# Cross-attention and gated feed-forward kernel: projections moved between a slot's score halves, a third projection bank, and softmax sums that share a bank and are added in SBUF

## Chip, core and metric

The kernel runs on one core of one Trainium2 chip, as one launch. The metric is device time in microseconds (us), from one launch to its end. The reference's numbers are fp32 throughout; there is no other core and no collective.

The engines are named as in the profile: PE (TensorE matmuls), PEld (its weight loads), DVE (VectorE), ACT (ScalarE), POOL (GpSimd) and SP (SyncE, which issues DMAs).

## The reference, cut to what matters

`x` is 4 batches of 256 tokens of 128 numbers, `ctx` 4 batches of 512 context rows of 128 numbers. Two layers follow each other for each batch.

```python
# layer 1: cross attention, 16 heads of 64
lat = layer_norm(layernorm(x)); ctx = layer_norm(context)
q = lat @ Wq                       # 256 x 1024
k, v = split(ctx @ Wkv)            # 512 x 1024 each
k = apply_rope(k, cos, sin)
attn = softmax(clip(q @ k.T * 64**-0.5, -11, 11))   # per head, 256 x 512
x = x + (attn @ v) @ Wo + bo

# layer 2: per-token attention over 16 heads of 8, then 8 gated experts
h = rmsnorm(layernorm(x)); q = h @ Wq + bq; kv = (h @ Wdown + bdown) @ Wup + bup
att = softmax(einsum('bthd,btgd->bthg', q, k) / sqrt(8))
y = layernorm(x) + (att @ v) @ Wo + bo
x = x + y + sum_e gate_e(h2) * (h2 @ We[e])         # h2 = rmsnorm(y)
```

## The kernel before

**Work and slots.** A slot is one pair of heads of one batch: 4 batches of 8 pairs give slots 0 to 31; p is the slot's number in its batch. Every engine has its own program, written out over the same list of slots (from -3 to 32), and semaphores tie them. Nothing is scheduled by a planner; the order is what the loops write, plus small tables (`POST_STEPS`, `OWN_STEPS`, `PREP_STEPS`) which say in which slot and at which place in it the steps of the second layer and the preparation of the next batch stand.

**One slot on PE.** With s the slot: `keys(s+3)` (three 512-column matmuls, K below), `scores(s, 0)` (12 matmuls on half the array's rows each, the first two of four context chunks), `queries(s+1)` (three 256-column matmuls, Q), in even slots `sums(s-1)` (16 matmuls of the softmax weights of two pairs with a column of ones), `scores(s, 1)`, `values(n)` (three 512-column matmuls, V; one unit in p = 1 to 4, two in p = 6 and 7, none in p = 0 and 5), and `times_values(s-1)` (8 matmuls, weights times values, called pv below). At places "a" (before Q), "b" (after V) and "c" (at the end) a side product can stand: `norm0` to `norm3`, `out_proj`, `h_T`, `query_down`, `keyval2`, `o_T`, `out_proj2`, `h2_T`, `gate`, `moe0` to `moe3` of the batch before, `ctx_T` and `lat_T` of the next.

**One slot on the others.** ACT takes the exponential of each score half (`exps`), both halves of which use the same two banks `sc`; so the second half's scores wait for the first half's exponential. It also copies queries (`query_hi`), values, rotated keys (`key_hi`) and pv (`attention_copy`, into `u`). POOL adds the rotary halves (`rotate`) and clips the exponentials (`clip`). DVE multiplies the key projection by sine and cosine (`key_products`, first in its slot), and makes the low parts `query_lo` and `key_lo` of the pair for the next slot; `scores(s+1, 0)` waits for both. Between the product with the sine and `rotate` SP issues four DMAs that swap halves.

**The second layer** of batch b runs beside the slots of batch b+1. From `keyval2` (p = 4) to `o_T` (p = 0 of the next batch) it is elementwise work on DVE and POOL: `products`, `sum_logits`, `less_maximum`, `weighted_values`, `reduce_outputs`. `o_T` on PE waits for it.

**Banks.** PSUM has eight banks here: `side`, two of `sc`, `own_bank`, two projection banks `pj_k`, `pv` and `sums`. K, Q and V units take the two projection banks in turn (`PLACE[...] % 2`), and `bank_free` waits for the reader of the unit two before. `sums` gathers the sums of four pairs of a batch's slots in one accumulation of 64 matmuls; `reciprocals(b)` on DVE reads them from there.

After slot 32 the last batch's second layer stands alone (`last_batches`, `TAIL_STEPS`); these last 54 us are called the tail.

Of the kernel before, what the change touches and what calls it, by code (L numbers as in the profile page):

```python
# [210 lines left out]
def xattn_ffn(nc, x, ctx, cos, sin, ln_lat_g, ln_lat_b, ln_ctx_g, ln_ctx_b, Wq, Wkv, Wo, bo,  # L211
              gamma1, f_Wq, f_bq, f_Wdown, f_bdown, f_Wup, f_bup, f_Wo, f_bo, gamma2, f_Wg, f_bg, f_We, out):
    es = ExitStack()
    with es:
# [73 lines left out]
        moe = sb("moe", [128, TT, NE, D])  # L288
        rec = sb("rec", [128, NT])
# [41 lines left out]
        first_value_banks = sc_bank + [pv_bank, sum_bank]  # L331
        side_banks = [pb("side")] + sc_bank + [own_bank] + pj_k + [pv_bank, sum_bank]
# [40 lines left out]
        s_u = sem("s_u")  # L373
        s_rec = sem("s_rec")
# [133 lines left out]
        def _(pe):  # L508
# [1106 lines left out]
```

## Time and profile before

| | us |
|---|---|
| median of 3 runs | 353.66 |
| lowest and highest | 352.28, 353.86 |
| profiled execution, its time | 351.67 |
| its span (first to last instruction) | 349.9 |
| mean granted TensorE clock | 0.943 |

| engine | busy us | share | instructions |
|---|---|---|---|
| PE | 299.8 | 86% | 2472 |
| DVE | 252.7 | 72% | 470 |
| POOL | 206.8 | 59% | 206 |
| ACT | 155.4 | 44% | 287 |

The share is a mean over stages: in slots 25 to 31 PE is busy almost throughout, between `keyval2` and `o_T` DVE is, and in the tail neither. The profile's chain of waits (the work that ended last, followed back) gives each piece its own share of the end, with the overlap of neighbouring matmuls taken off; the timeline gives start and full duration of each instruction. So a matmul of 400 ns in the timeline can be 230 ns of the chain.

### The profile page before, as it was taken

The page shows a single profiled execution, that of the slowest core. Times are in us where ns is not written, and L with a number is a line of the kernel's source. Part 1 is how long each engine was busy: PE and PEld are TensorE (multiplying, and loading weights), DVE is VectorE, ACT ScalarE, POOL GpSimd, SP SyncE. Part 2 cuts the span into 40 slices and gives each one's busy share as a digit, 9 for nine tenths or more (in the row PEclk, how much of TensorE's full clock was granted, in tenths as well). Part 3 has the DMA queues.
Part 4 walks back from the last instruction along what each step waited for, and adds up shares of the span by engine and source line. Part 5 has one row for each costly group of instructions (what it writes and reads, how often), then busy time and mean ns, then how long its engine had stood idle before and what let it go on. Part 6 is the DMA issues. An engine that isn't in the chain of part 4 may idle for free.

```text
span 349.9 us, 6553 instructions
## 1 busy us (share of the span) xinstructions
PE 299.8 (86%) x2472; PEld 198.7 (57%) x2472; DVE 252.7 (72%) x470; ACT 155.4 (44%) x287; POOL 206.8 (59%) x206
## 2 busy tenths in 40 slices
PE   6768999999999999959999999949999999740862
PEld 6545666666686655636776556627776555620331
DVE  3957635435866489997938689996456697799977
ACT  3536454565434545533336475624425665020420
POOL 4527744544656486773755586982544788754661
PEclk9989999999999999998999999978999999995668
DMA  8843212211111111111101020111101000000001
GB/s 230 232 120 81 51 30 63 61 31 34 30 32 32 30 33 32 31 30 32 32 7 42 13 51 11 32 31 32 32 17 46 15 2 3 15 0 0 0 2 30
DMA packets 16318, 14.23 MB, mean 41 GB/s; under 512 B 4832, under 2 KB 11808, under 8 KB 16288
## 3 DMA queue, kind: packets, MB, share of 16 engines
q1 hardware_dynamic: 15232, 13.69, 15.0%
q8 instruction: 20, 0.33, 0.4%
q10 hardware_dynamic: 1056, 0.13, 0.2%
q14 instruction: 10, 0.08, 0.1%
HBM read 4.89 MB, written 0.52 MB: 15 GB/s over the span
## 4 chain that ended last, share of the span: by engine, by line
PE 61%; DVE 26%; ACT 6%; issue 3%; DMA 2%; POOL 1%; SPq 0%; ACTq 0%; DVEq 0%; POOLq 0%
PE pv L587 16%; PE sc L573 14%; PE sums L603 6%; PE pj_k L511 6%; ACT e L794 5%; DVE o L1299 5%; PE pj_k L513 3%; PE pj_k L512 3%; PE side L674 3%; DVE att L1146 2%; DVE o L1302 2%; DVE ks L984 2%; DVE prod L967 2%; DMA sin_in<-in_L_xattn_sin_dram 2%; PE side L718 2%
## 5 line engine op out<-in xcount | busy, mean ns | idle before, releaser
L1488 POOL TENSOR_SCALAR e<-e 128x1024 f32<-128x1024 f32 x64 | 68.9, 1077 | 75.9 <-ACT e L794 68.3
L794 ACT ACTIVATE e<-sc 128x1024 f32<-128x1024 f32 x64 | 65.7, 1027 | 80.8 <-PE sc L573 80.8
L573 PE MATMUL sc<-qs,ks 64*128 64x256 f32 x768 | 63.1, 297 | 6.7 <-ACT e L794 6.0
L573 PEld LDWEIGHTS sc<-qs,ks 64*128 64x128 f32 x768 | 50.1, 187 | 29.4 <-issue 17.6
L587 PE MATMUL pv<-e,v 128*64 128x256 f32 x512 | 65.5, 400 | 0.0
L1481 POOL TENSOR_TENSOR krot<-kcos,kswap 128x512 f32<-128x512 f32 x32 | 41.2, 1288 | 17.0 <-DMA kswap<-ksin 8.9
L587 PEld LDWEIGHTS pv<-e,v 128*64 128x64 f32 x512 | 35.2, 142 | 24.4 <-issue 8.9
L1048 DVE TENSOR_TENSOR ksin<-pj_k,sinT 128x512 f32<-128x512 f32 x32 | 22.1, 690 | 34.6 <-PE pj_k L513 30.7
L984 DVE TENSOR_TENSOR ks<-krot,ks 128x512 fp32r<-128x512 f32 x32 | 33.4, 1043 | 0.0
L802 ACT ACTIVATE u<-pv 128x256 f32<-128x256 f32 x32 | 12.3, 385 | 43.4 <-PE pv L587 43.4
L603 PE MATMUL sums<-e,sum_rows 128*32 128x256 f32 x512 | 30.9, 382 | 0.0
L967 POOL TENSOR_TENSOR prod<-att,kv 128x1024 f32<-128x1024 f32 x8 | 23.4, 2937 | 6.6 <-ACT att L888 6.2
L959 POOL TENSOR_TENSOR prod<-q,kv 128x1024 f32<-128x1024 f32 x8 | 19.5, 2448 | 5.6 <-DVE kv L1179 3.5
L771 ACT ACTIVATE ks<-krot 128x512 fp32r<-128x512 f32 x32 | 20.1, 627 | 4.9 <-POOL krot L1481 4.9
L1048 DVE TENSOR_TENSOR kcos<-pj_k,cosT 128x512 f32<-128x512 f32 x32 | 21.8, 681 | 0.0
L984 DVE TENSOR_TENSOR qs<-pj_k,qs 128x256 fp32r<-128x256 f32 x32 | 13.4, 420 | 11.3 <-ACT qs L777 11.3
L603 PEld LDWEIGHTS sums<-e,sum_rows 128*32 128x32 f32 x512 | 15.0, 109 | 11.0 <-POOL e L1488 0.8
L1299 DVE TENSOR_REDUCE o<-prod 128x64 f32<-128x1024 f32 x16 | 18.8, 1207 | 0.1
L511 PE MATMUL pj_k<-ctxT,wkA 128*128 128x512 f32 x32 | 16.0, 501 | 3.0 <-DVE kcos L1048 2.8
L786 ACT ACTIVATE v<-pj_k 128x512 f32<-128x512 f32 x28 | 16.6, 594 | 1.9 <-PE pj_k L513 1.6
L1530 POOL TENSOR_TENSOR moe<-moe 128x512 f32<-128x512 f32 (+2 forms) x18 | 15.4, 854 | 2.7 <-ACT moe L869 1.8
L967 DVE TENSOR_TENSOR prod<-own_bank,kv 128x1024 f32<-128x1024 f32 x8 | 15.4, 1932 | 0.1
(257 smaller groups left out, 535.4 us busy)
## 6 DMA issues: line engine op xcount, KB each, us to landing
kswap<-ksin SPq DMA_DIRECT2D x128, 64.0 KB, 2.0
ctx_in<-in_ctx_dram SPq DMA_DIRECT2D x4, 256.0 KB, 3.0
prod<-in_L_xattn_Wkv_dram SPq DMA_DIRECT2D x2, 512.0 KB, 6.1
x_in<-in_x_dram SPq DMA_DIRECT2D x1, 512.0 KB, 6.0
prod<-in_L_xattn_Wq_dram SPq DMA_DIRECT2D x1, 512.0 KB, 6.8
wo<-in_L_xattn_Wo_dram SPq DMA_DIRECT2D x1, 512.0 KB, 8.3
fwe<-in_L_ffn_We_dram SPq DMA_DIRECT2D x1, 512.0 KB, 4.8
out_dram<-x_in SPq DMA_DIRECT2D x3, 128.0 KB, 1.8
```

The costliest lines, as they stand in the source:

```text
L511: nc.tensor.matmul(out_ap, w_hi, m_hi, start=True, stop=False)
L573: last = nc.tensor.matmul(sc[:, h, c * NT:(c + 1) * NT], ks[rows, j % 3, k_part, chunk], qs[rows, j % 2, q_part, :], start=(k_part + q_par ...
L587: last = nc.tensor.matmul(pv_bank[DH * h:DH * h + DH, 0:NT], v[:, c, col:col + DH], e[:, j % 3, h, c, :], start=(c == 0), stop=(c == SC - 1))
L603: last = nc.tensor.matmul(sum_bank[32 * g:32 * g + 32, 0:NT], w, e[:, (j - 1 + g // 2) % 3, g % 2, c, :], start=(p == 1 and c == 0), stop= ...
L771: nc.scalar.activation(ks[:, j % 3, 0, :], krot[:, j % 2, :], ACT.Copy).then_inc(s_khi, 1)
L794: nc.scalar.activation(e[:, j % 3, :, 2 * half:2 * half + 2, :].rearrange("p h c n -> p h (c n)"), sc[:, :, :], ACT.Exp, scale=SCALE).then ...
L967: return engine.tensor_tensor(prod[:, t, 1024 * hh:1024 * hh + 1024].rearrange("p (h d g) -> p h d g", h=G // 2, d=GD), weights(t)[:, 8 * ...
L984: return nc.vector.tensor_tensor(dst, whole, f(hi), ALU.subtract)
L1048: nc.vector.tensor_tensor(dst[:, j % 2, :], key_bank(j)[:, :], trig[:, :], ALU.mult).then_inc(s_kmul, 1)
L1299: return nc.vector.tensor_reduce(outputs(t)[:, 8 * hh:8 * hh + 8, :], pr, AX, ALU.add)
L1481: nc.gpsimd.tensor_tensor(krot[:, j % 2, :], kcos[:, j % 2, :], kswap[:, j % 2, :], ALU.add)\
L1488: nc.gpsimd.tensor_scalar(a, a, EXP_HIGH, EXP_LOW, ALU.min, ALU.max).then_inc(s_clip, 1)
```

## The change

- On PE a slot's order becomes `scores(s, 0)`, then in p = 0 `sums(s-1)`, then K, side "a", Q, V, side "b", `scores(s, 1)`, pv, in the other even slots `sums(s-1)`, side "c".
- ACT follows: values and side "b" are taken before the second exponential.
- There are three projection banks (`% 3`), and `bank_free` looks three units back. The first batch's fourth value unit uses `own_bank` and waits until `lat_T` is taken from it.
- `sums` no longer has a bank: it writes the other half of the pv bank (`sum_part`), one accumulation of 16 matmuls each. ACT copies each result to SBUF (`sums_copy`, into `sums_in`), 16 copies of 128x256. PE waits for that copy before the next pv or sums, and in odd pairs `attention_copy` waits for the sums that stand behind pv.
- POOL adds the second and third of a batch's four sums to the first (`add_sums`, in p = 5 and 7, 8 in all). DVE adds the fourth and takes the reciprocal from SBUF.

PE's program in slot 2, an even slot, before: K, first scores (L573), Q, sums, second scores, and the first row of V:

```order
52 L511 MATMUL pj_k<-ctxT,wkA 128x512
53 L512 MATMUL pj_k<-ctxT,wkA 128x512
54 L513 MATMUL pj_k<-ctxT,wkA 128x512
55 L573 MATMUL sc<-qs,ks 128x256 x12
56 L511 MATMUL pj_k<-latT,wqS 128x256
57 L512 MATMUL pj_k<-latT,wqS 128x256
58 L513 MATMUL pj_k<-latT,wqS 128x256
59 L603 MATMUL sums<-e,sum_rows 32x256 x16
60 L573 MATMUL sc<-qs,ks 128x256 x12
61 L511 MATMUL pj_k<-wvS,ctxT 128x512
```

The same slot on PE after the change, from the first scores (L579) to the sums (L614), with the middle of V left out:

```order
51 L579 MATMUL sc<-qs,ks 128x256 x12
52 L515 MATMUL pj_k<-ctxT,wkA 128x512
53 L516 MATMUL pj_k<-ctxT,wkA 128x512
54 L517 MATMUL pj_k<-ctxT,wkA 128x512
55 L515 MATMUL pj_k<-latT,wqS 128x256
56 L516 MATMUL pj_k<-latT,wqS 128x256
57 L517 MATMUL pj_k<-latT,wqS 128x256
58 L515 MATMUL pj_k<-wvS,ctxT 128x512
...
61 L579 MATMUL sc<-qs,ks 128x256 x12
62 L595 MATMUL pv<-e,v 64x256 x8
63 L614 MATMUL pv<-e,sum_rows 32x256 x16
```

All full-array products now stand together between the two halves, and sums stand behind pv.

PE's program in slot 16 before, where `o_T` (the transposes of o) waits for DVE's second layer:

```order
262 L603 MATMUL sums<-e,sum_rows 32x256 x16
263 L573 MATMUL sc<-qs,ks 128x256 x12
264 L610 MATMUL side<-ident,o 128x128 x2
265 L587 MATMUL pv<-e,v 64x256 x8
266 L705 MATMUL side<-fwo,oT 128x128 x2
267 L511 MATMUL pj_k<-ctxT,wkA 128x512
```

And the same place after:

```order
261 L517 MATMUL pj_k<-latT,wqS 128x256
262 L621 MATMUL side<-ident,o 128x128 x2
263 L579 MATMUL sc<-qs,ks 128x256 x12
264 L595 MATMUL pv<-e,v 64x256 x8
265 L714 MATMUL side<-fwo,oT 128x128 x2
266 L579 MATMUL sc<-qs,ks 128x256 x12
```

The second score half of the slot moves from ahead of the waiting transposes to behind them.

POOL's program from slot 31 on after the change (clips, an addition of sums, then a product of the second layer); before, the clips were followed by the product:

```order
151 L1514 TENSOR_SCALAR e<-e 128x2x512 x2
152 L1518 TENSOR_TENSOR sums_in<-sums_in 128x256
153 L991 TENSOR_TENSOR prod<-att,kv 128x1024
154 L1562 TENSOR_TENSOR moe<-moe 128x512
155 L1562 TENSOR_TENSOR moe<-moe 128x256
```

One addition stands ahead of the product that DVE's last addition of sums meets.

```diff
@@ PE, the loop over slots
             for slot in range(-KEYS_AHEAD, AFTER):
+                if 0 <= slot < NPAIR:
+                    scores(slot, 0)
+                if slot > 0 and slot % PAIRS == 0:
+                    sums(slot - 1)
                 if slot + KEYS_AHEAD < NPAIR:
                     keys(slot + KEYS_AHEAD)
-                if 0 <= slot < NPAIR:
-                    scores(slot, 0)
                 side_at(slot, "a")
                 if 0 <= slot + 1 < NPAIR:
                     queries(slot + 1)
-                if 2 <= slot <= NPAIR and slot % 2 == 0:
-                    sums(slot - 1)
-                if 0 <= slot < NPAIR:
-                    scores(slot, 1)
                 for n in value_units(slot):
                     values(n)
                 side_at(slot, "b")
+                if 0 <= slot < NPAIR:
+                    scores(slot, 1)
                 if 1 <= slot <= NPAIR:
                     times_values(slot - 1)
+                if 2 <= slot < NPAIR and slot % 2 == 0 and slot % PAIRS:
+                    sums(slot - 1)
                 side_at(slot, "c")
@@ PE, times_values
                 if j:
                     pe.wait_ge(s_u, j)
+                if j > 1:
+                    pe.wait_ge(s_sums_copied, (j + 1) // 2 if p == PAIRS - 1 else j // 2)
@@ PE, sums
-                if p == 1 and b:
-                    pe.wait_ge(s_rec, b)
+                pe.wait_ge(s_u, j)
+                if j > 1:
+                    pe.wait_ge(s_sums_copied, j // 2)
@@ PE, bank_free
-                if PLACE[kind, n] < 2:
+                if PLACE[kind, n] < 3:
                     return
-                kind, n = PROJECTIONS[PLACE[kind, n] - 2]
+                kind, n = PROJECTIONS[PLACE[kind, n] - 3]
@@ ACT
+            def sums_copy(j):
+                act.wait_ge(s_sum, j // 2 + 1)
+                if j >= PAIRS:
+                    act.wait_ge(s_rec, j // PAIRS)
+                nc.scalar.activation(sums_in[:, j % PAIRS // 2, :], sum_part, ACT.Copy).then_inc(s_sums_copied, 1)
             def attention_copy(j):
                 act.wait_ge(s_pv, j + 1)
+                if j % 2 and j % PAIRS != PAIRS - 1:
+                    act.wait_ge(s_sum, j // 2 + 1)
@@ DVE
             def reciprocals(b):
-                dve.wait_ge(s_sum, PAIRS // 2 * (b + 1))
-                nc.vector.reciprocal(rec[:, :], sum_bank[:, 0:NT]).then_inc(s_rec, 1)
+                dve.wait_ge(s_sums_added, 2 * b + 2)
+                dve.wait_ge(s_sums_copied, PAIRS // 2 * (b + 1))
+                own(nc.vector.tensor_tensor(rec[:, :], sums_in[:, 0, :], sums_in[:, 3, :], ALU.add))
+                nc.vector.reciprocal(rec[:, :], rec[:, :]).then_inc(s_rec, 1)
@@ POOL
+            def add_sums(b, i):
+                pool.wait_ge(s_sums_copied, PAIRS // 2 * b + i + 1)
+                nc.gpsimd.tensor_tensor(sums_in[:, 0, :], sums_in[:, 0, :], sums_in[:, i, :], ALU.add)\
+                    .then_inc(s_sums_added, 1)
+                pool.wait_ge(s_sums_added, 2 * b + i)
@@ POOL, in each slot, behind the second clip
+                if 0 <= b < NB and p in (5, 7):
+                    add_sums(b, p // 2 - 1)
```

## Rows read from the trace of the kernel before

**Rows 1.** Busy time by stage: start:end, length, PE, PEld, DVE, ACT, POOL, PEclk, DMA.
```profile
25.18:95.00 69.82, 66.56 (x611) 44.30 (x612) 38.23 (x77) 37.42 (x61) 37.05 (x35) 0.99 0.20 50
95.00:122.90 27.90, 27.33 (x253) 19.42 (x253) 16.08 (x38) 12.81 (x21) 15.07 (x18) 1.00 0.12 29
122.90:156.40 33.50, 28.08 (x264) 18.07 (x263) 32.11 (x40) 16.26 (x28) 24.96 (x17) 1.00 0.13 32
196.00:233.40 37.40, 31.73 (x271) 19.42 (x271) 34.38 (x40) 20.63 (x44) 30.78 (x25) 0.98 0.12 29
233.40:293.20 59.80, 58.93 (x513) 39.13 (x513) 41.10 (x71) 29.18 (x55) 34.79 (x35) 0.96 0.08 21
293.20:350.00 56.80, 31.01 (x152) 17.91 (x152) 46.77 (x100) 11.01 (x37) 32.13 (x36) 0.77 0.03 8
```

**Rows 2.** Chain that ended last, slots 2 to 7: start us, us, engine, tile, line.
```profile
37.77 0.32 PE pj_k L511
38.32 1.86 PE sums L603 x32
40.18 0.91 PE sc L573 x12
41.09 0.43 PE pj_k L511
41.99 1.88 PE pv L587 x16
...
44.75 0.93 PE sc L573 x10
45.70 1.03 ACT e L794
46.78 0.98 PE sc L573 x12
...
66.82 0.12 PE pj_k L511
...
70.83 0.23 PE pj_k L511
```

**Rows 3.** Timeline, DVE, POOL and PE in the stretches 123 to 156 and 196 to 233 us.
```profile
127.98 0.42 DVE L984 TENSOR_TENSOR qs<-pj_k,qs 128x256 fp32r<-128x256 f32 x1 [0.55 <-ACT qs L777]
148.67 2.91 POOL L967 TENSOR_TENSOR prod<-att,kv 128x1024 f32<-128x1024 f32 x1
149.00 2.73 DVE L1302 TENSOR_TENSOR o<-o,aden 128x128 f32<-128x128 f32 x1
156.39 0.60 PE L610 MATMUL side<-ident,o 128*128 128x128 f32 x2 [3.75 <-DVE o L1302]
206.60 0.69 DVE L1048 TENSOR_TENSOR ksin<-pj_k,sinT 128x512 f32<-128x512 f32 x1 [0.96 <-PE pj_k L513]
233.42 0.66 PE L610 MATMUL side<-ident,o 128*128 128x128 f32 x2 [4.73 <-DVE o L1302]
```

**Rows 4.** Busy time and granted clock (behind POOL's figure) behind the first of PE's two waits.
```profile
157.00:160.50 3.50, 3.50 (x18) 1.90 (x19) 2.84 (x4) 0.52 (x2) 1.95 (x2) 0.59 0.02 5
```

**Rows 5.** Timeline, DVE in slot 19: first key product and low part of the keys.
```profile
181.45 0.69 DVE L1048 TENSOR_TENSOR ksin<-pj_k,sinT 128x512 f32<-128x512 f32 x1 [1.71 <-PE pj_k L513]
185.53 1.55 DVE L984 TENSOR_TENSOR ks<-krot,ks 128x512 fp32r<-128x512 f32 x1
```

**Rows 6.** Timeline, slots 0 and 1: a cast on DVE, scores that wait for ACT.
```profile
26.39 0.68 DVE L1400 CAST spread<-u 128x1024 fp32r<-128x1024 f32 x1
30.13 0.97 PE L573 MATMUL sc<-qs,ks 64*128 64x256 f32 x12 [0.31 <-ACT e L794]
```

**Rows 7.** Timeline, end of the slots: clip and product on POOL, reciprocal on DVE.
```profile
292.49 1.04 POOL L1488 TENSOR_SCALAR e<-e 128x1024 f32<-128x1024 f32 x1 [1.10 <-ACT e L794]
293.61 2.89 POOL L967 TENSOR_TENSOR prod<-att,kv 128x1024 f32<-128x1024 f32 x1
296.23 1.76 DVE L1060 RECIPROCAL rec<-sums 128x256 f32<-128x256 f32 x1 [1.94 <-PE sums L603]
```

More of the change, by code:

```diff
@@ L288, in xattn_ffn @@
         moe = sb("moe", [128, TT, NE, D])
+        sums_in = sb("sums_in", [128, PAIRS // 2, NT])
         rec = sb("rec", [128, NT])
@@ L321, in xattn_ffn @@
         own_bank = pb("own_bank")
-        pj_k = [pb(f"pj_k{i}") for i in range(2)]
+        pj_k = [pb(f"pj_k{i}") for i in range(3)]
         pv_bank = pb("pv")
-        sum_bank = pb("sums")
+        sum_part = pv_bank[:, NT:2 * NT]
         q2_bank = own_bank[:, 0:D]
         att_bank = own_bank[:, NT:2 * NT].rearrange("p (h g) -> p h g", h=G)
-        first_value_banks = sc_bank + [pv_bank, sum_bank]
-        side_banks = [pb("side")] + sc_bank + [own_bank] + pj_k + [pv_bank, sum_bank]
+        first_value_banks = sc_bank + [pv_bank, own_bank]
+        side_banks = [pb("side")] + sc_bank + [own_bank] + pj_k[0:2] + [pv_bank, pj_k[2]]
         ld = {n: sem(f"ld_{n}") for n in ("wk", "trig", "x", "wv", "wq", "bias", "wo", "ffn")}
@@ L373, in xattn_ffn @@
         s_u = sem("s_u")
+        s_sums_copied = sem("s_sums_copied")
+        s_sums_added = sem("s_sums_added")
         s_rec = sem("s_rec")
@@ L436, in value_bank @@
         def value_bank(n):
-            return first_value_banks[n] if value_units_at_first(n) else pj_k[PLACE["values", n] % 2]
+            return first_value_banks[n] if value_units_at_first(n) else pj_k[PLACE["values", n] % 3]
         def key_bank(j):
-            return pj_k[PLACE["keys", j] % 2]
+            return pj_k[PLACE["keys", j] % 3]
         def query_bank(j):
-            return pj_k[PLACE["queries", j] % 2]
+            return pj_k[PLACE["queries", j] % 3]
         def weights(t):
@@ L551, in values @@
                     pe.wait_ge(s_wv, 1)
+                if n == 3:
+                    pe.wait_ge(*taken("lat_T", 0))
                 if not value_units_at_first(n):
@@ L602, in sums @@
                     for g in range(4):
-                        last = nc.tensor.matmul(sum_bank[32 * g:32 * g + 32, 0:NT], w,
+                        last = nc.tensor.matmul(sum_part[32 * g:32 * g + 32, :], w,
                                                 e[:, (j - 1 + g // 2) % 3, g % 2, c, :],
-                                                start=(p == 1 and c == 0), stop=(p == PAIRS - 1 and c == SC - 1))
+                                                start=(c == 0), stop=(c == SC - 1))
                 last.then_inc(s_sum, 1)
@@ L638, in side_product @@
                     pe.wait_ge(s_u, NPAIR)
-                elif k == 7:
-                    pe.wait_ge(s_rec, NB)
-                elif k >= 4:
+                elif k >= 4 and k != 6:
                     pe.wait_ge(s_qlo, NPAIR)
@@ L914, in _ @@
                     exps(slot, 0)
+                if slot > 0 and slot % PAIRS == 0:
+                    sums_copy(slot - 1)
                 side_taken(slot, "a")
@@ L917, in _ @@
                     query_hi(slot + 1)
+                for n in value_units(slot):
+                    value_copy(n)
+                side_taken(slot, "b")
                 if 0 <= slot < NPAIR:
                     exps(slot, 1)
-                for n in value_units(slot):
-                    value_copy(n)
                 if 0 <= slot + KV_AHEAD < NPAIR:
                     key_hi(slot + KV_AHEAD)
-                side_taken(slot, "b")
                 if 1 <= slot <= NPAIR:
                     attention_copy(slot - 1)
+                if 2 <= slot < NPAIR and slot % 2 == 0 and slot % PAIRS:
+                    sums_copy(slot - 1)
                 second_layer(slot, "c")
```

2 lines of the change are left out of this document (1 added, 1 removed).

## Prediction, made blind

> **What bounds the kernel now.** I read the busy time by stage first. From 25 to 123 us and from 233 to 293 us PE is busy nearly throughout (66.56 of 69.82, 27.33 of 27.90, 58.93 of 59.80 us) and DVE well below it [rows 1]. In two stretches, 123 to 156 and 196 to 233 us, it is the other way round: DVE is busy 32.11 of 33.50 and 34.38 of 37.40 us, and at their end PE stands idle for 3.75 and 4.73 us in front of `o_T` [rows 1, 3]. So there are two regimes: slots that PE bounds (2 to 12, 17 to 20, 25 to 31) and two stretches that DVE bounds (13 to 16, 21 to 24). A change on PE pays in the first only. The tail (293 to 350 us, PE 31 of 57 us, DVE 47) is a chain over DVE, PE and ACT which the change leaves alone but for its first link.
>
> Then I read the chain of waits inside PE's slots, for what a slot costs there [rows 2]. First scores 0.91, pv 1.88, sums 1.86. A full-array projection costs 0.43+0.23+0.23=0.89 behind scores or pv, but 0.69 behind another full-array product (its first matmul falls from 0.43 to 0.23). Q costs 0.32+0.12+0.12=0.56 behind scores and 0.36 behind another product. In odd slots nothing but Q lies between the halves, and PE waits for the exponential: 46.78 less 45.68 us, which is 1.10 us, the exponential's 1.03 among it, and then 0.98 for the second half.
>
> **The change on PE's slots.** Even slot before: K 0.89, scores 0.91, Q 0.56, sums 1.86, scores 0.91, V 0.89, pv 1.88, in all 7.90. After: scores 0.91, K 0.89, Q 0.36, V 0.69, scores 0.91, pv 1.88, sums 1.86, in all 7.50: a gain of 0.40. Odd slot before: 0.89+0.93+1.10+0.98+0.89+1.88=6.67. After: the projections (1.94) cover the exponential, 0.91+0.89+0.36+0.69+0.91+1.88=5.64: a gain of 1.03. Slot 5 has no V: 0.82, K and Q (1.25) still covering the 1.10. With two V: 1.04. With p=0: 0.20. Slot 9 has norms in the old gap, which is thus half used: 0.61. Slot 10 has a side product behind pv already: 0.19.
>
> The gain in 0.20 steps is a count of how often PE goes from full-array matmuls to half- or part-array ones: seven changes in an even slot, five after. The Trainium skill, TensorEngine Tiling (Array Packing), Key Properties, says that changing the tiling mode drains the engine. By that rule the new neighbours pv and sums, which tile differently, cost a drain too. The trace shows sums at 1.86 behind a full-array product, where such a change is in it already, so the sum is the same by both; the pair pv, sums itself stands in no row.
>
> Slots 2 to 11: 0.40+1.03+0.40+0.82+0.40+1.04+0.20+0.61+0.19+1.04, which is **-6.1**.
>
> Slots 0 and 1: K(3) used to lie ahead of the first scores, in a wait. Now DVE gets it only after them; its products (1.3), the cast (0.68 [rows 6]), `query_lo` and `key_lo` (1.1) follow one another, and scores(1, 0) starts at about 31.1 instead of 30.13 [rows 6]: **+0.9** with what slot 1 saves again.
>
> **The stretches that DVE bounds.** DVE works in order, and its slot begins with `key_products(s+3)`, which now wait for a K that stands behind the first scores. `keyval2` comes sooner, but DVE then waits for K(16) at the head of slot 13, so nothing of that is kept: +0.3. Inside, waits for Q fall away (0.55 in slot 13 [rows 3] and 0.23 in slot 15) and PE is never late. Stretch 1: **-0.8**. Stretch 2 has such a gap of 0.96, a wait for K [rows 3], and two more for Q of together 1.4; half of the 2.4 goes: **-1.2**. Bounds for each: nothing, and -2.0 if also the 2.73 us of DVE's small product (L1302, which ends as POOL's 2.91 us product does [rows 3]) shrinks.
>
> **Behind `o_T`.** PE now waits with the second scores of the slot still to do. Before, `o_T` 0.6, pv, `out_proj2` and K followed; now `o_T`, scores, pv, `out_proj2`: +0.2 at full clock. The granted clock behind the wait was 0.59 of full, mostly its lower level of 1.2 GHz, until about 160.5 us [rows 4]; PE idled 3.75 us before that. The wait gets longer (about 6 us), and the work in the low clock now counts scores too: the slot after begins at 162.2 to 162.8 instead of 160.96. **+1.5** and, behind the second wait, **+1.3**; bounds 0.2 and 2.5 each.
>
> **Slots 17 to 20 and 25 to 28.** Here DVE is loaded as well. In slot 19 from the first key product to `key_lo` it takes 185.53+1.55-181.45=5.63 us [rows 5]. K is ready 1.8 us after a slot's start (0.7 before), plus 0.1, so a slot with this chain lasts at least 7.55. Slot 19 took 7.28 and gets +0.3; slot 27 took 6.84 with the same chain and gets +0.7; in slot 11 the chain is 4.5, and the slot keeps its gain. Slots 17 to 20: -0.61-0.19+0.3, **-0.5**. Slots 25 to 28: -0.61-0.19+0.7-0.40, **-0.5**.
>
> **Slots 29 to 32.** No K stands here. Slot 29 gains 0.8 (`moe0` moves into the gap). Slot 30 loses what sums used to cover: Q's 0.56 is all there is against 1.10, +0.6. Slot 31 stays. In slot 32 sums no longer stand behind `moe3`, but need the last clip (1.04 us, its exponential ahead of it [rows 7]); then a copy (0.39, as u's) and DVE's addition (0.42, as its 128x256 sums): the reciprocal could start 0.1 later than 296.23. **-0.1** in all.
>
> **The new work.** 16 copies on ACT (6.2 us; ACT is at half load): copies of u and sums behind sums(s-1) end 0.85 us later, while scores(s+1, 0) take 0.91, so the next exponential is not held. 8 additions on POOL of 0.73 each; POOL's product in slot 15 ended some 2 us before DVE needed it, so they are hidden; without that cover they would cost up to 0.7 per stretch. DVE's three inner additions lie in slots 8, 16 and 24, off PE's path. The last does not: POOL's product ran from 293.61 for 2.89 us [rows 7], starts 0.7 later behind `add_sums` and lasts to 297.2. The small DVE product of [rows 3] shows what an operation of DVE with two SBUF inputs does under such a product: it ended when the product did. So the addition, due at 295.8, ends about 1.2 later: **+1.2**, bounds 0 and 1.5. The Trainium skill, SBUF — State Buffer, Who interferes with whom, states it as a rule: DVE with two SBUF inputs contends with a GpSimd instruction that reads SBUF. It speaks against this change, and the trace agrees. With no such contention the sum would be 1.2 better.
>
> **Waits that it adds.** pv waits for the copy of the sums before; it comes 3.7 us after it. The second of two V waits for the key products of its own slot: 0.2 where DVE is free, hidden where it is not. `sums` of slots 16 and 24 now stand ahead of K and need a clip behind POOL's 3 us product: K is still there before DVE asks.
>
> **Sum:** +0.9-6.1-0.8+1.5-0.5-1.2+1.3-0.5-0.1+1.2 is -4.3 us. Against the profiled execution: span 349.9 to 345.6, its time 351.67 to 347.4. The median stands 2.0 above that execution, so I forecast **349.4**.
>
> **Rivals.**
> - *DVE's stretches and the last addition go well.* Both stretches gain their 2.0, the addition finds POOL free, the clock recovers as before: -1.2-2.0-1.5=-4.7 more, **344.7**. For: gaps of that size are there. Against: DVE is at 96% in the first. Chance 0.18.
> - *PE's whole gain arrives.* The same arithmetic for all 32 slots gives -13.5, **340.2**. It needs DVE's stretches to shrink with PE's, against 32.11 of 33.50 us busy. Chance 0.05.
> - *Slower: K comes too late for DVE.* Where DVE's chain from K to `key_lo` is longer than the slot less 1.8 us, the slot grows. I count that for slots 19 and 27. There are ten other loaded slots (9 to 12, 17, 18, 20, 25, 26, 28); each that tips over turns about -0.5 into +0.7. From five on the kernel is at **355.4** and slower; all ten give 361. The chain has 4.5 us against 6.45 in slot 11, and slots 10, 12, 18, 20 are longer still, which is against it; that DVE has 0.2 to 0.9 us more in some of them under POOL's additions speaks for it. Chance 0.11.
> - *The change does little:* low clock after more of the waits in the stretches (up to +2.5 each) with the rest as summed, near **353**. For: PE idles more and in more places there. Chance 0.14.
>
> **How the numbers follow.** The forecast holds 0.52, its own range 346.5 to 352. The range 344 to 355.5 leaves out the full gain and most of the slower rival. A measurement of this kernel can tell about 0.5% (1.8 us) from no change: 351.9 and 355.4 are the borders. Faster 0.71 (forecast most of it, the first two rivals), same 0.16 (the little one and the forecast's upper end), slower 0.13.
>
> **What would show it.** In the profile after: no wait of the second scores for the exponential in slots 2 to 29; odd slots of some 5.7 us and even ones of 7.5 in slots 2 to 8; the start of slot 12 about 5.2 us earlier; `o_T` waits longer than 3.75 and 4.73 us, at 150.5 and about 227 us; a reciprocal that starts 3 to 4 us earlier than 296.23 behind an addition of about 1.5 us. It is wrong if the odd slots do not shorten, if PE's waits for `ks` spread over many slots, or if the low clock is seen away from `o_T`.

## The result and the profile after

| | before | after |
|---|---|---|
| median, us | 353.65 (4 runs) | 360.22 (4 runs) |
| lowest and highest | 352.28, 353.86 | 359.20, 362.31 |
| ratio, 95% interval | | 1.0198, 1.0165 to 1.0230 |
| span of the profiled run | 349.9 | 360.5 |
| mean granted clock | 0.943 | 0.917 |

The kernel became 2% slower, 10.8 us above the forecast and 4.7 above the range. The profiled execution of after is its slowest; the spans of the other three are 357.4, 357.5 and 359.3 us. What is said of stages below holds for the profiled executions.

The table sets the profiled executions side by side. A stage is measured from first scores to first scores; the second and third columns are after less before, as the prediction's sum had it and as measured.

| stage | before, us | forecast | measured |
|---|---|---|---|
| slots 0, 1 | 11.61 | +0.9 | +3.38 |
| 2 to 5 | 28.69 | -2.65 | -2.72 |
| 6, 7 | 16.13 | -1.44 | -0.26 |
| 8 | 7.00 | -0.20 | -0.18 |
| 9 to 11 | 26.84 | -1.84 | +1.16 |
| 12 to 15 (DVE's stretch 1) | 32.89 | -0.8 | +1.05 |
| 16 (behind `o_T`) | 13.24 | +1.5 | +1.59 |
| 17 to 20 | 37.14 | -0.5 | +2.47 |
| 21 to 24 (stretch 2, `o_T`) | 40.59 | +0.1 | -1.83 |
| 25 to 28 | 35.81 | -0.5 | +1.85 |
| 29 to the tail's first norm | 24.36 | +1.1 | +1.79 |
| tail | 50.4 | 0 | +2.2 |

The forecast's two stretches end at the transposes of `o_T`, inside slots 16 and 24. Cut there, slots 12 to 16 up to the transposes came out at +2.03 (forecast -0.8) and what is behind them at +0.61 (forecast +1.5); slots 21 to 24 up to the transposes at -1.88 (forecast -1.2) and what is behind them at +0.05 (forecast +1.3). So slot 16 agrees in the table because two errors offset each other.

The busy time hardly changed (PE 300.2 us, 299.8 before; DVE 248.8, 252.7 before); the waits did. The groups of instructions by line, DVE's product with the sine (the first thing that waits for K), in after and then in before (columns: count, busy, mean ns, idle time before them and what ended it):

```profile
L1072 DVE TENSOR_TENSOR ksin<-pj_k,sinT 128x512 f32<-128x512 f32 x32 | 22.1, 689 | 70.1 <-PE pj_k L517 57.4 <-POOL krot L1507 12.7
```
```profile
L1048 DVE TENSOR_TENSOR ksin<-pj_k,sinT 128x512 f32<-128x512 f32 x32 | 22.1, 690 | 34.6 <-PE pj_k L513 30.7 <-POOL krot L1481 3.6
```

DVE's idle time in front of K doubled, 34.6 to 70.1 us, at unchanged work. Most of it costs nothing; where it costs shows in the waits of PE. The timeline of after, PE's waits at side products that before has not, in slots 9, 10, 12, 17 to 20, 25 and 26:

```profile
92.29 0.36 PE L674 MATMUL side<-recS,spread 128*128 128x256 f32 x1 [1.49 <-issue]
102.08 3.84 PE L683 MATMUL side<-wo,on 128*128 128x128 f32 x32 [0.52 <-DVE on L1123]
121.74 0.70 PE L707 MATMUL side<-fwup,dT 64*128 64x256 f32 x2 [0.68 <-DVE q L1137]
169.62 0.38 PE L674 MATMUL side<-recS,spread 128*128 128x256 f32 x1 [0.52 <-DVE on L1123]
178.05 3.84 PE L683 MATMUL side<-wo,on 128*128 128x128 f32 x32 [0.91 <-DVE on L1123]
191.26 0.66 PE L621 MATMUL side<-ident,ctx_n 128*128 128x128 f32 x4 [1.07 <-DVE gl L1154]
199.79 0.70 PE L707 MATMUL side<-fwup,dT 64*128 64x256 f32 x2 [0.66 <-DVE q L1137]
247.99 0.38 PE L674 MATMUL side<-recS,spread 128*128 128x256 f32 x1 [0.52 <-DVE on L1123]
256.88 3.84 PE L683 MATMUL side<-wo,on 128*128 128x128 f32 x32 [1.38 <-DVE on L1123]
```

The first has another cause: `recS`, from the reciprocals of the batch, stands on DVE behind the key products and the low parts of slot 8, and those wait for a K and a Q that now come behind scores and sums. Before, the reciprocal started at 85.24, 3.6 us into the slot, and slot 9's norm waited for nothing. In after it starts 6.4 us in. With K ahead (e2 below) it still starts 5.2 us in, since DVE then waits 2.39 us for Q. Timeline of after, DVE:

```profile
85.95 0.69 DVE L1072 TENSOR_TENSOR ksin<-pj_k,sinT 128x512 f32<-128x512 f32 x1 [6.65 <-PE pj_k L517]
88.09 0.42 DVE L1085 TENSOR_TENSOR rec<-sums_in 128x256 f32<-128x256 f32 x1
90.66 1.53 DVE L1008 TENSOR_TENSOR recS<-rec,recS 128x256 fp32r<-128x256 f32 x1
```

All others in the list stand at side place "b" and are released by DVE's taking of side "a" of the same slot. How that comes about, in slot 18 of after (timeline, PE and DVE):

```profile
173.74 0.98 PE L579 MATMUL sc<-qs,ks 64*128 64x256 f32 x12
175.22 0.39 PE L517 MATMUL pj_k<-ctxT,wkA 128*128 128x512 f32 x1
175.45 0.28 PE L674 MATMUL side<-recS,spread 128*128 128x256 f32 x1
175.72 0.69 DVE L1072 TENSOR_TENSOR ksin<-pj_k,sinT 128x512 f32<-128x512 f32 x1 [1.11 <-PE pj_k L517]
176.33 0.68 DVE L1072 TENSOR_TENSOR kcos<-pj_k,cosT 128x512 f32<-128x512 f32 x1
176.93 0.47 DVE L1353 TENSOR_SCALAR hn<-xl,rr 128x128 f32<-128x128 f32 x2
177.31 0.68 DVE L1123 TENSOR_TENSOR on<-u,side 128x512 f32<-128x512 f32 x1
178.05 3.84 PE L683 MATMUL side<-wo,on 128*128 128x128 f32 x32 [0.91 <-DVE on L1123]
```

DVE idles 1.11 us for K, whose last matmul ends 1.9 us into the slot. Its two key products and `hn` come ahead of `on`, in DVE's own order. PE has meanwhile done side "a", Q and V (to 177.1) and stands at side "b", which needs the single `side` bank and `on`. In before, 170.09 to 170.9 for the same norm, DVE took it at 170.95, and the sums (1.93), the second scores and V lay between "a" and "b" (174.67, no wait). So both edits meet: K later by the first scores, and "b" nearer to "a" by the second scores and by sums or, in odd slots, the wait for the exponential.

A third kind of wait is new: the second V of a slot stands until DVE has taken K with its cosine product. The wait is 0.42 us in slot 7 and 1.24, 0.70 and 0.80 in slots 14, 15 and 22; before, V waited there for the low part of Q, 0.52 us in slot 14 and 0.39 in slot 22. Timeline of after, slot 14:

```profile
138.02 0.50 PE L515 MATMUL pj_k<-wvS,ctxT 128*128 128x512 f32 x1 [1.24 <-DVE kcos L1072]
```

The start. PE's first scores of after, then the first scores of slot 1, from the timeline:

```profile
25.27 1.65 PE L579 MATMUL sc<-qs,ks 64*128 64x256 f32 x12 [5.50 <-DVE ks L1008]
31.93 1.65 PE L579 MATMUL sc<-qs,ks 64*128 64x256 f32 x12 [1.21 <-ACT e L805]
```

Before, K(3) filled part of that wait and the scores of slot 1 took 0.97 [rows 6]; in after they take 1.65, at a granted clock of 0.50 (1.2 GHz), which lasts from 24.4 to 38.1 us.

The second edge, `o_T`, and the end of the slots (timeline of after; compare [rows 3] and [rows 7]):

```profile
159.89 0.66 PE L621 MATMUL side<-ident,o 128*128 128x128 f32 x2 [4.93 <-DVE o L1328]
238.12 0.66 PE L621 MATMUL side<-ident,o 128*128 128x128 f32 x2 [4.06 <-DVE o L1328]
303.05 1.33 DVE L1085 TENSOR_TENSOR rec<-sums_in 128x256 f32<-128x256 f32 x1 [1.94 <-ACT sums_in L812]
307.87 0.55 PE L674 MATMUL sc<-recS,spread 128*128 128x256 f32 x1 [2.46 <-DVE recS L1008]
```

### The profile page after: what moved, and what is told of

Read it like the earlier page. It is cut to its first block, busy times and chain, and to the rows that moved or that the text cites. A ratio compares the mean times of both kernels' runs of the same rounds, so it can differ in the third digit from the quotient of the medians.

```text
span 360.5 us, 6653 instructions
## 1 busy us (share of the span) xinstructions
PE 300.2 (83%) x2472; PEld 206.5 (57%) x2472; DVE 248.8 (69%) x474; ACT 163.3 (45%) x303; POOL 212.0 (59%) x214
## 4 chain that ended last, share of the span: by engine, by line
PE 52%; DVE 29%; POOL 6%; issue 5%; ACT 3%; DMA 3%; SPq 1%; ACTq 0%; DVEq 0%; POOLq 0%
PE sc L579 13%; PE pv L595 12%; PE pv L614 6%; PE pj_k L515 4%; DVE o L1325 4%; PE side L683 3%; DVE ksin L1072 3%; DVE kcos L1072 3%; DVE ks L1008 3%; PE pj_k L517 3%; PE pj_k L516 3%; DVE prod L991 2%; POOL e L1514 2%; POOL krot L1507 2%; PE side L621 2%
## 5 line engine op out<-in xcount | busy, mean ns | idle before, releaser
L579 PE MATMUL sc<-qs,ks 64*128 64x256 f32 x768 | 68.0, 310 | 9.2 <-DVE ks L1008 6.9
L579 PEld LDWEIGHTS sc<-qs,ks 64*128 64x128 f32 x768 | 54.2, 198 | 29.4 <-issue 13.7
L1072 DVE TENSOR_TENSOR ksin<-pj_k,sinT 128x512 f32<-128x512 f32 x32 | 22.1, 689 | 70.1 <-PE pj_k L517 57.4
L595 PE MATMUL pv<-e,v 128*64 128x256 f32 x512 | 64.7, 396 | 0.0
L1008 DVE TENSOR_TENSOR ks<-krot,ks 128x512 fp32r<-128x512 f32 x32 | 32.3, 1009 | 0.0
L614 PE MATMUL pv<-e,sum_rows 128*32 128x256 f32 x512 | 30.9, 382 | 0.5 <-POOL e L1514 0.5
L614 PEld LDWEIGHTS pv<-e,sum_rows 128*32 128x32 f32 x512 | 15.2, 109 | 14.1 <-issue 4.2
L788 ACT ACTIVATE qs<-pj_k 128x256 fp32r<-128x256 f32 x32 | 12.4, 386 | 13.2 <-PE pj_k L517 13.0
L1562 POOL TENSOR_TENSOR moe<-moe 128x512 f32<-128x512 f32 (+2 forms) x18 | 14.9, 826 | 2.5 <-ACT moe L889 1.4
```

The costliest lines, as they stand in the source:

```text
L579: last = nc.tensor.matmul(sc[:, h, c * NT:(c + 1) * NT], ks[rows, j % 3, k_part, chunk], qs[rows, j % 2, q_part, :], start=(k_part + q_par ...
L595: last = nc.tensor.matmul(pv_bank[DH * h:DH * h + DH, 0:NT], v[:, c, col:col + DH], e[:, j % 3, h, c, :], start=(c == 0), stop=(c == SC - 1))
L614: last = nc.tensor.matmul(sum_part[32 * g:32 * g + 32, :], w, e[:, (j - 1 + g // 2) % 3, g % 2, c, :], start=(c == 0), stop=(c == SC - 1))
L1008: return nc.vector.tensor_tensor(dst, whole, f(hi), ALU.subtract)
L1072: nc.vector.tensor_tensor(dst[:, j % 2, :], key_bank(j)[:, :], trig[:, :], ALU.mult).then_inc(s_kmul, 1)
```

## The experiments

Theory T: the time is lost to the order, through a K that DVE gets late and a side "b" that follows "a" closely. Rivals: the new banks and the path of the sums cost it (S); the low clock at the start and behind the waits costs it (C). Ratios are to the kernel before, with their 95% intervals.

**Order or banks.** `e3_order_only` is the kernel before with the new order, `e4_banks_only` the new banks and path of sums with the old order.

```diff
@@ e3_order_only: two banks and a bank for sums stay
+                if 0 <= slot < NPAIR:
+                    scores(slot, 0)
+                if slot > 0 and slot % PAIRS == 0:
+                    sums(slot - 1)
                 if slot + KEYS_AHEAD < NPAIR:
                     keys(slot + KEYS_AHEAD)
...
                 side_at(slot, "b")
+                if 0 <= slot < NPAIR:
+                    scores(slot, 1)
```

> The kernel before with the new order of PE and ACT alone: K, Q, V and sides between the halves and sums behind pv, but two projection banks, sums in their own bank in one accumulation of 64 matmuls, no copies and no additions. Theory 'the order costs it, through K's place': about as slow as the changed kernel or slower, 360 to 363, since with two banks every V must wait for the key products of its own slot. Rival 'the sums' new path costs it': back at the forecast, 349 to 352.

> The changed kernel with PE and ACT in the order of before (K, scores, Q, sums, scores, V, pv): three banks, shared sums bank, 16 copies, 8 additions on POOL and 4 on DVE alone. Theory 'the order costs it': near the kernel before, 353.7 plus 1.3 (last addition behind POOL) less up to 1.5 (V no longer waits for the low part of Q in slots 14 and 22), 352.5 to 356. Rival 'the sums' new path costs it': 358 to 361.

Measured: order alone 376.32 us, 1.0619 (1.0572 to 1.0667), 13 us above what was expected; banks alone 350.34 us, 0.9895 (0.9853 to 0.9936). S falls: with the old order the banks and the sums' path cost nothing in all. In e4 slots 16 and 24 take 10.60 and 13.84 us instead of 13.24 and 15.78, and slots 12 to 15 and 21 to 23 take 0.8 and 0.7 less. Slot 31 to the first norm takes 1.0 more (the last addition) and the tail 0.9, the other stages from slot 2 on stay within 0.15. The gain of 1% is not the banks' alone: behind `o_T` of slot 16 the clock stayed at 1.00 here and fell to 0.50 in before. The order costs 2.8% on top of them and 6% without them: with two banks the V behind K and Q needs a bank that DVE has not read. The timeline of e3, slots 14 and 15, DVE's idle time and the V that waits:

```profile
146.21 0.80 PE L511 MATMUL pj_k<-wvS,ctxT 128*128 128x512 f32 x1 [2.26 <-DVE qs L986]
155.40 0.69 DVE L1050 TENSOR_TENSOR ksin<-pj_k,sinT 128x512 f32<-128x512 f32 x1 [5.42 <-PE pj_k L513]
```

**K's place.** `e2_keys_first` is after with one statement moved; `e5_k_first_p0` does it in slots 8, 16 and 24 alone, `e6_k_first_not_p0` in all others.

```diff
@@ PE, the loop over slots
+                if slot + KEYS_AHEAD < NPAIR:
+                    keys(slot + KEYS_AHEAD)
                 if 0 <= slot < NPAIR:
                     scores(slot, 0)
                 if slot > 0 and slot % PAIRS == 0:
                     sums(slot - 1)
-                if slot + KEYS_AHEAD < NPAIR:
-                    keys(slot + KEYS_AHEAD)
```

> The changed kernel with one thing undone: K stands ahead of the first scores again in every slot (and so ahead of sums in p = 0); Q, V and side b stay between the halves, three banks and shared sums stay. Theory 'DVE in its order gets K too late': the start comes back (-4.3), the norm slots 9, 10, 17, 18, 25, 26 lose the 7.7 us that they ran over the forecast, the first DVE stretch its 2.2; against it stand 0.2 us per slot for one more change of tiling (5.6) and 0.54 in each of three p = 5 slots: some 360.2-14+7 = 353, with a gain of 7 in all. Rival theory 'shared sums bank and the extra work of ACT, POOL and DVE cost it': K's place does not matter, the time stays at 360 plus the 7 us of tiling changes, 365 or so.

> The changed kernel (360.2 us) with K ahead of the first scores and of sums in slots 8, 16 and 24 alone. Theory 'the norm slots': there K stands behind scores and sums (2.8 us later than before), DVE begins its slot 2.8 us later, the reciprocal and norm0 with it, and slots 9, 10, 17, 18, 25, 26 grow by 7.7 us over the forecast. Then this one edit brings back most of that, 5 to 6 us: 354 to 355. Rival theory 'K is late in every slot alike': three slots of 32 give about a tenth to a fifth of the 9 us that all together gave, 358.5 to 359.5.

> The complement: K ahead of the first scores in every slot but 8, 16 and 24. Theory 'the norm slots': only the rest of the 9 us comes back, 3 to 4 us: 356 to 357. Rival 'in every slot alike': 352 to 353.

Measured: 351.17 us, 0.9915 (0.9877 to 0.9953); 358.58, 1.0162 (1.0099 to 1.0224); 351.02, 0.9934 (0.9911 to 0.9956). One statement is worth 9 us, 8.2 of it from slot 2 to the first norm. Moved in all slots but 8, 16 and 24 it gives 9.2, more than either theory had. In slots 8, 16 and 24 alone it gives 1.6, within the spread of the executions, and its slots from 2 on take 1.1 us more than those of after: the theory that the late K of these three slots is what costs the norm slots (354 to 355 us) falls. By stage, e2 against after: slots 0 and 1 -2.23 (in part the clock, see the start below), slots 2 to 5 +1.49 (the change's order pays there), 6 and 7 -0.74, 8 +0.19, 9 to 11 -1.21, 12 to 15 -2.28, 16 -1.87, 17 to 20 -1.56, 21 to 24 +0.37, 25 to 28 -2.54. Yet e2 is no faster than e4 with the old order (350.34): what its order gains in slots 2 to 7 (2.2 us) and in single slots later it loses again in slots 9, 16, 24 and 30 (in slot 16 with the clock's part). DVE's idle time before the sine product falls with it (groups by line, e2):

```profile
L1072 DVE TENSOR_TENSOR ksin<-pj_k,sinT 128x512 f32<-128x512 f32 x32 | 22.0, 687 | 42.2 <-PE pj_k L517 38.4 <-POOL krot L1507 3.6
```

**Side "b".** `e12_b_behind_scores` leaves K late and moves only "b" behind the second scores, in slots with p = 1 to 4 from slot 9 on.

```diff
@@ PE, the loop over slots (ACT follows)
-                side_at(slot, "b")
+                if not late_b(slot):
+                    side_at(slot, "b")
                 if 0 <= slot < NPAIR:
                     scores(slot, 1)
+                if late_b(slot):
+                    side_at(slot, "b")
```

> The changed kernel (360.22) with side product b behind the second scores in slots with p = 1 to 4 from slot 9 on (norm1, out_proj, ctx_T, keyval2), K left where the change put it. Theory 'side product b stands too close behind a, and DVE takes a only after the late key products': PE's waits of 0.5 to 0.7 us at b in slots 12, 17, 20 and 25 fall away, and slots 10, 18 and 26 lose their 0.5 to 1.4: 357 (356 to 358.5). Rival 'DVE's own chain behind the late K sets these slots, wherever PE waits': the waits move to the next scores, and the time stays at 360 within 1.

Measured: 353.73 us, 0.9999 (0.9975 to 1.0023), 6.5 under after and below the 356 to 358.5 of the theory. Against after, slots 9 to 11 take 0.52 less, 17 to 20 2.04, 25 to 28 1.99, slots 12 to 16 0.33; slot 24 takes 0.83 more. Slots 17, 19, 20 and 26 take 7.47, 7.27, 9.58 and 12.18 instead of 8.05, 8.17, 10.30 and 13.57. The rival (DVE's chain sets these slots wherever PE waits) falls. Its DVE still idles 63.0 us in front of K:

```profile
L1106 DVE TENSOR_TENSOR ksin<-pj_k,sinT 128x512 f32<-128x512 f32 x32 | 22.1, 690 | 63.0 <-PE pj_k L532 55.5 <-POOL krot L1541 7.4
175.31 3.84 PE L699 MATMUL side<-wo,on 128*128 128x128 f32 x32 [1.08 <-DVE on L1157]
```

So in slots 17 to 20 and 25 to 28 a late K costs mostly because side "b" waits behind it. In slot 18 itself the wait stays (the second row) and the slot takes 13.25. Only in DVE's first stretch, slots 12 to 15, is K's place the cause by itself (33.86 with "b" moved, 31.66 with K moved). Slot 9 keeps its wait for `recS` (1.49 us). The two profiled executions are 7.8 us apart: 4.1 between slot 9 and the first norm, the rest at the start and in the tail, where the same instructions ran at another clock. So 4.1 us are shown to be the edit's; the other 2.4 of the 6.5 between the medians are not.

**The start.** `e1_warm` puts 22 matmuls of 128 columns, whose result nobody reads, into the free `side` bank ahead of scores(0, 0).

> The changed kernel (360.2 us) with 22 dummy 128x128 matmuls on PE into the side bank, right before the first scores of slot 0, where PE stood idle for 5.5 us; nothing reads them. Theory 'clock': slots 0 and 1 ran at the granted clock 0.50 until 37 us because PE idled before them, and slot 2 began at 40.26 instead of the 36.9 of the forecast. Then slot 2 begins at about 36.9 and the kernel takes 3.4 us less, 356.8. Theory 'DVE gets K(3) late': only the order counts there, dummy matmuls change nothing or less than 0.5 us.

Measured: 360.72, 1.0200 (1.0161 to 1.0238). The clock was 1.00 in 20 to 33 us as intended, and the median gained nothing. PE then waited 2.94 us for DVE in slot 1 (first row, e1), and behind that wait the clock was at 0.50 from 33.3 to 36.7; the two slots took 13.20 us. That K's products are late is so at either clock; rival C falls as the cause of the whole, though this run is no clean test, since the low clock came back in slot 1. How much of the +3.38 is the execution's own shows in e12, whose program is that of after up to slot 8: the same 5.50 us wait, but the clock back at 1.00 at 31.2 instead of 38.1 us (second and third row, e12), and 12.28 us for both slots, +0.67.

```profile
32.75 1.21 PE L579 MATMUL sc<-qs,ks 64*128 64x256 f32 x12 [2.94 <-DVE ks L1012]
```
```profile
25.62 1.65 PE L594 MATMUL sc<-qs,ks 64*128 64x256 f32 x12 [5.50 <-DVE ks L1042]
32.27 0.98 PE L594 MATMUL sc<-qs,ks 64*128 64x256 f32 x12 [1.21 <-ACT e L831]
```

**`o_T`, and an order for each slot.** `e7_oT_behind_scores` is e2 with `o_T` of slots 16 and 24 behind the second scores. `e8_mixed` takes the change's order in slots 2 to 5, the old place of the second scores in twelve slots with side products or loaded DVE (8, 9, 14 to 17, 19, 20, 23, 24, 26, 30), and e2's elsewhere.

> The kernel with K first everywhere (351.2 us), and in slots 16 and 24 the transposes of o, which wait for DVE, stand behind the second scores again. Theory 'the wait holds the scores': PE has 0.9 us more to do before the wait and the same less behind it, part of it at the granted clock 0.5: 1.2 to 2.4 us less per place, 347 to 349. Rival 'DVE ends last there in any case': the stretch is DVE's, the scores go into the wait for nothing, 350.5 to 351.5.

> One banks-and-sums scheme (that of the changed kernel), the order chosen per slot from the slot lengths measured in four kernels: the changed order in slots 2 to 5, the order of before in 8, 9, 14 to 17, 19, 20, 23, 24, 26, 30, and K first with the rest as changed elsewhere. If slot lengths add up where PE bounds and DVE's stretches absorb the rest: 3.7 us off slots 2 to 7, 1.3 off 10 to 12, 0.4 to 0.8 in each of 27, 28 and 29 against the kernel with the order of before (350.3): 343.5 to 346. If a slot's length depends on the slot before it (DVE's lag carried on): 347 to 350.

Measured: 346.45, 0.9825 (0.9774 to 0.9876), and 344.47, 0.9733 (0.9693 to 0.9774). Both are faster than either kernel. `o_T` of slot 16 in e2, then in e7:

```profile
154.26 0.66 PE L621 MATMUL side<-ident,o 128*128 128x128 f32 x2 [3.62 <-DVE o L1328]
```
```profile
151.39 0.41 PE L637 MATMUL side<-ident,o 128*128 128x128 f32 x2 [2.72 <-DVE o L1362]
```

The wait is 0.9 us shorter because the second scores (0.98) now lie ahead of it. Slots 16 and 24 take 0.74 and 1.93 less than in e2; another 1.7 of the 4.7 us is in slots 0 and 1, whose program is the same (the clock was low until 34.7 us in e2 and until 29.1 in e7).

**The last addition.** `e9_sum_from_psum` is e8 with the fourth part of the last batch's sums read from PSUM by DVE, without ACT's copy; the other batches keep the old addition.

```diff
@@ DVE, reciprocals, last batch
-                own(nc.vector.tensor_tensor(rec[:, :], sums_in[:, 0, :], sums_in[:, 3, :], ALU.add))
+                    nc.vector.tensor_tensor(rec[:, :], sum_part, sums_in[:, 0, :], ALU.add).then_inc(s_sums_copied, 1)
```

> The mixed order (344.47), and the last addition of sums takes its fourth part straight from PSUM instead of from SBUF; ACT's copy of it (0.38 us) is left out. Theory 'POOL's product holds a DVE operation with two SBUF inputs': with one input in PSUM the addition falls from 1.41 to about 0.42 us beside the same POOL product (2.9 us), and the reciprocal starts 1.5 us earlier (0.4 for the copy, 1.0 for the addition): 343.0. Rival 'the addition is slow for another reason, its place behind the small operations or the low clock': it stays at 1.4 us, only the copy is saved: 344.0.

Measured: 343.78, 0.9703 (0.9658 to 0.9747), against e8's 344.47: not told apart by the time. The timelines do, e8 first, then e9 (POOL's product, the addition of sums, POOL's next additions, the cast, the low part; the reciprocal between takes 1.75 in both):

```profile
283.61 2.91 POOL L1028 TENSOR_TENSOR prod<-att,kv 128x1024 f32<-128x1024 f32 x1
285.40 1.41 DVE L1122 TENSOR_TENSOR rec<-sums_in 128x256 f32<-128x256 f32 x1 [0.99 <-ACT sums_in L841]
287.19 2.60 POOL L1599 TENSOR_TENSOR moe<-moe 128x512 f32<-128x512 f32 x3 [0.67 <-ACT moe L918]
288.63 0.78 DVE L1125 CAST recS<-rec 128x256 fp32r<-128x256 f32 x1
289.44 0.63 DVE L1045 TENSOR_TENSOR recS<-rec,recS 128x256 fp32r<-128x256 f32 x1
```
```profile
284.15 2.91 POOL L1030 TENSOR_TENSOR prod<-att,kv 128x1024 f32<-128x1024 f32 x1
285.52 0.42 DVE L1125 TENSOR_TENSOR rec<-pv,sums_in 128x256 f32<-128x256 f32 x1 [0.59 <-PE pv L633]
287.73 2.66 POOL L1606 TENSOR_TENSOR moe<-moe 128x512 f32<-128x512 f32 x3 [0.68 <-ACT moe L920]
287.76 1.39 DVE L1132 CAST recS<-rec 128x256 fp32r<-128x256 f32 x1
289.19 0.90 DVE L1047 TENSOR_TENSOR recS<-rec,recS 128x256 fp32r<-128x256 f32 x1
```

Under the same product the addition takes 0.42 with an operand in PSUM and 1.41 with both in SBUF: the contention of the forecast is shown, at 1.0 us. But the gain is mostly lost two instructions later: the cast and the low part take 1.39 and 0.90 instead of 0.78 and 0.63. Both run beside POOL's additions in either kernel; in e9 the cast starts with the first of them, in e8 1.4 us later. What there holds it is not shown. From slot 31 to the first norm it is 12.27 instead of 12.80 us, a gain of 0.5.

**The clock.** `e10_clock` is e8 with 11 and 13 such idle matmuls ahead of the two `o_T`; `e11_both` has these, e9's edit, and 14 ahead of the tail's first norm.

```diff
@@ PE, side_product, ahead of the waits for the source
+                for _ in range(({0: 11, 1: 13}.get(b, 0) if name == "o_T" else 0)):
+                    nc.tensor.matmul(side[:, 0:128], ident[:, :], ident[:, :], start=True, stop=True)
```

> The mixed order (344.47) with 11 and 13 idle matmuls of 128 columns into the free side bank ahead of o_T of slots 16 and 24, where PE waits for DVE; no result changes. The granted clock was 0.66 in 150 to 154 us and 0.50 in 224 to 228 us. Theory 'behind a wait it is the low clock that lengthens the slot': the clock stays near 1.00 behind both, slots 16 and 24 lose about 1 and 2 us: 341.5 (340.5 to 342.5). Rival 'DVE (busy 3.90 and 3.97 of 4.00 us there) sets that stretch, PE's clock is free': slots 16 and 24 as before, 344.5.

> Both edits, and 14 idle matmuls ahead of the first norm of the tail as well, where PE waits 2.46 us for recS and the norms then run at 0.41 instead of 0.28 us each. If the low clock costs in all three places and the contended addition too: 344.5-1.5-3.0-0.8 is 339.2. If only the addition counts: 343.0. If only the clock counts: 340.7.

Measured: 341.74, 0.9658 (0.9605 to 0.9712); 340.31, 0.9648 (0.9585 to 0.9710). The intervals overlap each other and, just, that of e8, so the stages have to tell. Busy time and granted clock (behind POOL's figure) behind `o_T`, e8 and then e10:

```profile
150.00:154.00 4.00, 3.88 (x21) 2.27 (x22) 3.90 (x6) 0.77 (x2) 2.85 (x3) 0.66 0.02 4
224.00:228.00 4.00, 3.87 (x18) 2.01 (x18) 3.97 (x4) 0.38 (x1) 3.84 (x4) 0.50 0.06 15
```
```profile
150.00:154.00 4.00, 3.97 (x34) 2.80 (x33) 3.93 (x7) 1.05 (x3) 3.12 (x4) 1.00 0.14 34
224.00:228.00 4.00, 4.00 (x31) 2.60 (x33) 3.96 (x4) 0.77 (x2) 3.84 (x4) 1.00 0.03 6
```

Slots 16 and 24 fall from 12.21 to 10.57 and from 14.90 to 12.16, though DVE was busy 3.90 and 3.97 of 4.00 us: C is right about these two places, 1.6 and 2.7 us of low clock. Behind the second, slots 25 to 28 take 1.75 more (36.55 instead of 34.80), 1.51 of it in new waits for DVE in slot 25, so of the 2.7 only 1.0 stays. In e11 the tail from the first norm takes 50.4 us, as before, instead of 52.7 in e8. Its 14 matmuls were too many, though: they end after `recS` is ready (286.9) and hold the first norm to 288.18. Its median lies nearer to the 340.7 of the clock alone than to the 339.2 of all three.

## Why the prediction was wrong

- **PE's slots, 2 to 8**: right to 0.1 us (slots 2 to 5: 7.49, 6.06, 7.49, 4.93, forecast 7.50, 6.09, 7.50, 4.96), except slots with two V. There the forecast put the wait of the second V at 0.2 and otherwise counted it hidden. It was 0.20 and 0.42 in slots 6 and 7 (part of what these slots took over the sum: 8.87 us instead of 8.34 and 7.00 instead of 6.35), and where DVE is loaded it was not hidden at all: 1.24, 0.70 and 0.80 in slots 14, 15 and 22.
- **Slots 9 to 11, 17 to 20, 25 to 28**: the failed step, 8.3 of the 14.9 us by which the profiled span exceeds the forecast one. The forecast asked whether DVE's chain from K to `key_lo` fits the slot, and priced that (slots 19 and 27). The chain did fit; slot 27 even took 6.47. What failed stands between: side "a" is taken behind the key products, and side "b" waits for that. The prediction counted "b" as moving with V at no cost. Slots 17 to 20 came out at 39.61 us where the sum gave 36.6, 25 to 28 at 37.66 where it gave 35.3; with K ahead (e2) they take 38.05 and 35.12, with "b" later (e12) 37.58 and 35.67. In slots 9 to 11 2.2 of the 3.0 us are slot 9's, where it is the late `recS`: K's place gives 0.7 of it (8.54 in e2), the order of K, Q and sums the rest (7.75 in e8, with the old order in slots 8 and 9). The rival "K comes too late for DVE" named the late K, and its 355.4 to 361 holds the measured time, but by another way (a chain to `key_lo` longer than the slot), and with the start and the tail in the measured time; that its size fits is in part luck. Its evidence against itself (chain 4.5 of 6.45 us in slot 11) was about that chain, not the one that cost.
- **Stretch 1**: forecast -0.8, measured +1.05 in slots 12 to 15 and +2.03 up to the transposes. That PE is "never late" there was wrong. With K ahead, e2 has -1.23 against before in slots 12 to 15. **Stretch 2**: forecast -1.2, measured -1.88 up to the transposes, so this half was nearly right. In slot 13 of after DVE idles 3.20 us for K, and the first scores of slot 14 then wait for `ks` (timeline):

```profile
129.25 0.69 DVE L1072 TENSOR_TENSOR ksin<-pj_k,sinT 128x512 f32<-128x512 f32 x1 [3.20 <-PE pj_k L517]
133.65 0.98 PE L579 MATMUL sc<-qs,ks 64*128 64x256 f32 x12 [1.39 <-DVE ks L1008]
```

- **Behind `o_T`**: slot 16 as a whole was +1.59 for a forecast of +1.5, which is luck: 0.98 of it lies ahead of the transposes, and behind them it is +0.61 there and +0.05 in slot 24, for +1.5 and +1.3. The forecast's term has a slip of 0.7 in it: 160.96 is where the next slot's K started in before, and it was compared with the start of first scores in after; those of before started at 161.65 in the same chain. And the waits went from 3.75 to 4.93 and from 4.73 to 4.06 us, not to 6. That the low clock has such a price e10 shows (1.6 in slot 16 of e8), but before had a stretch at 0.50 behind both waits already, 3.4 and 6.8 us long, against 6.9 and 6.9 in after.
- **Start**: +0.9 forecast, +3.38 measured. The four profiled executions with a late K there (after, e3, e5, e12) took 13.62 on average, +2.0, and the three with three banks grow with the time at which the clock came back: 12.28 (31.2 us), 13.67 (35.3) and 14.99 (38.1). With K ahead and the clock back at 31.8 to 33.3 us, e8, e9 and e10 took 10.93 to 11.18. An estimate from these and e12 is that the late K is worth 1.1 to 1.4 us there; the forecast's size was sound, and what it left out is the low clock, up to 2.7.
- **Last addition**: 1.33 us instead of 0.42, as forecast (0.9 of contention for a forecast of 1.2; from slot 31 to the norm it is +1.57). **Tail**: counted as untouched, measured +2.2. 1.3 of it are the norms at the low clock (0.41 us each instead of 0.28); e2 and e12, with the norms at full clock, have 51.3. The other 0.9 goes with a later stretch at 0.50, 20.5 us long in after, e2 and e12 and 17.1 in before and in e11, whose tail is 50.4 again; that it is this stretch is argued, not shown.
- **Total**: of the 14.9 us between the forecast span (345.6) and the profiled one, 8.3 are in slots 9 to 11, 17 to 20 and 25 to 28, 1.9 in slots 12 to 15, 1.2 in slots 6 and 7, 2.5 at the start, 2.9 from slot 29 on, and -1.9 in slots 21 to 24 (0.7 up to the transposes, 1.2 behind them).

Open: why stretch 2 gained where stretch 1 lost. And of slots 17 to 20 and 25 to 28 it is shown that either edit (K ahead, "b" later) gives the time back: in 25 to 28 to within 0.4 us of the forecast, in 17 to 20 to within 0.9 to 1.4 us. It is not shown how it divides between them, since no run makes both in all these slots.

## What to carry over

When a producer is moved later on one engine, follow every instruction that stands behind its consumer in the consumer's order, not only the chain that the product itself feeds; then look for who waits for those. Closing a gap on the fast engine also removes the distance between two uses of one bank; ask at each such pair whether the reader of the first still gets there in time. An order that pays in one kind of slot can be taken there alone: the mixed one is 2.7% faster than before where the uniform one is 2% slower.

## What was not expected of the hardware

- The same program with the same wait (5.50 us before the first scores) ran at the low clock (0.50) until 38.1 us in one execution (after) and until 31.2 us in another (e12); slots 0 and 1 took 14.99 and 12.28 us.
- Waits of 2.7 us can leave the clock at 1.00 (e4 in 156 to 160 us, behind 2.74 us) or not (e8 in 150 to 154 us: 0.66, behind the same 2.74 us); a wait of 3.75 us left 0.59 [rows 4]. Idle matmuls in the wait kept it at 1.00 behind that wait each time (e1, e10, e11); in e10 the medians are 2.7 us apart (344.47 and 341.74), near the edge of what four executions tell, and slots 16 to 28 take 2.6 us less.
- A DVE cast from SBUF to SBUF of 128x256 took 1.39 us when it started with POOL's additions (e9) and 0.78 when it came 1.4 us after their start (e8).
